# Attention values as the stationary operand, with the two terms moved through two column halves of the array

## What is computed

```python
scores = ttt_filter(q @ k.T / 8)                # [1024, 1024] per head
attn = softmax(scores)
attn = attn * (sin(C1*attn) * exp(-attn*attn/PHI) + cos(C2*attn))
ctx = attn @ v                                  # [1024, 64]
h = h + concat(ctx) @ Wo + bo
```

## Time and profile before

| | |
|---|---|
| runs shown, us | 6780.7, 6791.86, 6778.62 |
| time of the profiled execution, us | 6774.6 |
| its span, us | 6772.9 |
| mean granted TensorE clock | 0.892 of 2.4 GHz |
| TensorE matmul busy, us | 5442.1 (80%) |
| weight load busy, us | 3955.2 (58%) |
| VectorE busy, us | 5082.3 (75%) |
| ScalarE busy, us | 4262.2 (63%) |
| GpSimd busy, us | 2754.5 (41%) |
| of it GpSimd's sum L377, 1024 of 1272 ns, us | 1289.3 |
| values matmuls L635, 8192 records, busy us | 1162.6 |

### The profile page before, as it was taken

One profiled execution on the slowest core, in us unless ns is written; L12 is line 12 of the kernel. 1 busy time (PEld: TensorE's weight loads), 2 busy tenths in 40 slices (PEclk: granted clock), 3 DMA queues, 4 the chain that ended last, 5 costly groups with the idle time before them and its releaser, 6 DMA issues. The chain is left out here.

```text
span 6772.9 us, 115321 instructions
## 1 busy us (share of the span) xinstructions
PE 5442.1 (80%) x32426; PEld 3955.2 (58%) x32489; DVE 5082.3 (75%) x10177; ACT 4262.2 (63%) x7370; POOL 2754.5 (41%) x2639
## 2 busy tenths in 40 slices
PE   2788877787777877877888777778787799997999
PEld 1455555555555555555655555555555577775777
DVE  1888888888888888888888888888888555555443
ACT  1677777777777777777777777777777322222222
POOL 4445554444555544444555444445554200100111
PEclk9888898989889888888888889888988799898999
DMA  1000000000000000000000000000000000000000
GB/s 17 12 8 7 7 7 7 7 7 10 7 7 7 7 7 7 7 9 9 7 7 7 7 7 7 9 9 7 7 7 4 8 1 2 1 1 13 4 6 6
DMA packets 34500, 48.46 MB, mean 7 GB/s; under 512 B 24473, under 2 KB 24537, under 8 KB 34010
## 3 DMA queue, kind: packets, MB, share of 16 engines
q1 hardware_dynamic: 31962, 43.49, 2.5%
q0 software_dynamic: 2048, 0.14, 0.1%
HBM read 39.40 MB, written 4.19 MB: 6 GB/s over the span
## 5 line engine op out<-in xcount | busy, mean ns | idle before, releaser
L571 PE MATMUL banks<-ident,att 128*128 128x128 f32 x8192 | 1458.9, 311 | 873.6 <-DVE ag L508 496.8
L571 PEld LDWEIGHTS banks<-ident,att 128*128 128x128 f32 x8192 | 1024.2, 159 | 1568.6 <-DVE ag L508 1044.0
L377 POOL TENSOR_TENSOR sinb<-sinb,work 128x512 f32<-128x512 f32 x1024 | 1289.3, 1272 | 900.3 <-DVE sinb L482 898.3
L599 PE MATMUL banks<-kT,qT 128*128 128x512 f32 x2048 | 1262.5, 702 | 113.9 <-ACT att L423 104.0
L387 POOL TENSOR_SCALAR wgt<-wgt 128x512 f32<-128x512 f32 x1024 | 700.2, 684 | 1586.7 <-DVE wgt L502 1581.4
L635 PEld LDWEIGHTS outp<-vo,sinb 128*128 128x128 f32 x8192 | 1164.7, 216 | 214.9 <-issue 185.3
L635 PE MATMUL outp<-vo,sinb 128*128 128x64 f32 x8192 | 1162.6, 295 | 1.9 <-ACT att L423 1.9
L476 DVE TENSOR_TENSOR work<-banks,work 128x512 f32<-128x512 f32 x1024 | 699.8, 689 | 254.0 <-ACT work L435 183.6
L451 ACT ACTIVATE work<-banks 128x512 f32<-128x512 f32 x1024 | 609.9, 596 | 420.4 <-PE banks L571 411.6
L458 ACT ACTIVATE mag<-banks 128x512 f32<-128x512 f32 x1024 | 606.4, 594 | 356.2 <-PE banks L599 350.0
L435 ACT ACTIVATE work<-banks,halfpi 128x512 f32<-128x512 f32 x1024 | 695.4, 685 | 208.9 <-PE banks L571 139.6
(11 more groups left out here) (194 smaller groups left out, 6740.6 us busy)
## 6 DMA issues: line engine op xcount, KB each, us to landing
xq<-xT_dram SPq DMA_DIRECT2D x64, 256.0 KB
xv<-xT_dram SPq DMA_DIRECT2D x64, 256.0 KB, 3.7
xT_dram<-xT SPq DMA_DIRECT2D x8, 256.0 KB, 2.9
out<-hres SPq DMA_DIRECT2D x8, 256.0 KB, 2.6
base<-in_L_tok_turns,idx POOLq DMA_INDIRECT x64
wqk<-in_L_attn_Wq SPq DMA_DIRECT2D x64, 16.0 KB
wqk<-in_L_attn_Wk SPq DMA_DIRECT2D x64, 16.0 KB
wqk<-in_L_attn_bq SPq DMA_DIRECT2D x64, 0.2 KB
```

The costliest lines, as they stand in the source:

```text
L377: nc.gpsimd.tensor_tensor(sinb[:, k % RING], sinb[:, k % RING], work[:, k % RING], ALU.add).then_inc(summed, 1)
L571: mm = nc.tensor.matmul(bank[:, i * P:(i + 1) * P], att[:, p, 4 * half + i, kt * P:(kt + 1) * P], ident[:], is_transpose=True, start=(i == ...
L599: nc.tensor.matmul(score_bank(n), qT[:, p, (n // 2) * P:(n // 2 + 1) * P], kT[:, p, (n % 2) * 512:(n % 2 + 1) * 512], start=True, stop=Tru ...
```

## The change

- The values matmuls swap operands: `vo[:, kt]` (128x64) is stationary, and 512 columns are moved, once from `work` (cosine term) and once from `sinb` (sine term). The first writes partitions 0 to 63 of `outp`, the second 64 to 127: the built program gives them the tile 128x64 of the array at column 0 and at column 64. `outp` then holds output features by queries, for one half of the queries at a time.
- GpSimd's sum L377 is gone. ScalarE and VectorE wait for `av` where they waited for `summed`.
- The tiles go through the keys of the first query half, then of the second: `kt = k % TB`, `half = k // TB`. `AV` is one per step for the first eight (steps 34 to 41), every second step for the last eight (steps 0, 2, ... 14 of the next iteration).
- VectorE empties `outp` twice per head (steps 42 and 15): copied into `acc` for an even head, added to `acc` for an odd one. After the odd head TensorE folds `acc` back with eight 128x64 matmuls against `pair` (two stacked identities), and VectorE adds the result to `hres`. `PROJ` moves from step 18 to 19.
- `qT` and `kT` are no longer padded. Even heads lie on partitions 0 to 63, odd heads on 64 to 127, and the score matmul contracts 64 rows (tile 64x128 of the array, at row 0 or 64).

```diff
-        AV = [SINE + 6 + 8 * k // 5 for k in range(NTILE)]
-        OUT = AV[-1] + 1
+        AV = [SINE + 6 + k if k < TB else SINE + 16 + 2 * (k - TB) for k in range(NTILE)]
+        OUT = (AV[TB - 1] + 1, AV[-1] + 1)
+        FOLD, ADD = OUT[1] + 1, OUT[1] + 2
...
-                            wait(pool, tmul, NTILE * g + k + 1)
-                            nc.gpsimd.tensor_tensor(sinb[:, k % RING], sinb[:, k % RING], work[:, k % RING],
-                                                    ALU.add).then_inc(summed, 1)
...
-                        if a == OUT:
-                            wait(dve, av, NTILE * (g + 1))
+                        if a in OUT:
+                            half = OUT.index(a)
+                            wait(dve, av, NTILE * g + TB * (half + 1))
+                            if p == 0:
+                                nc.vector.tensor_copy(acc[:, half], outp[:]).then_inc(evac, 1)
+                            else:
+                                nc.vector.tensor_tensor(acc[:, half], outp[:], acc[:, half], ALU.add).then_inc(evac, 1)
+                        if a == ADD and p == 1:
+                            wait(dve, folded, folds(g, p) + 1)
...
-                            nc.tensor.matmul(score_bank(n), qT[:, p, (n // 2) * P:(n // 2 + 1) * P],
-                                             kT[:, p, (n % 2) * 512:(n % 2 + 1) * 512],
+                            rows = slice(p * D, (p + 1) * D)
+                            nc.tensor.matmul(score_bank(n), qT[rows, (n // 2) * P:(n // 2 + 1) * P],
+                                             kT[rows, (n % 2) * 512:(n % 2 + 1) * 512],
...
-                            wait(pe, summed, NTILE * g + k + 1)
+                            kt, half = k % TB, k // TB
+
+                            wait(pe, acd, NTILE * g + k + 1)
+                            wait(pe, tmul, NTILE * g + k + 1)
                             if k == 0:
                                 wait(pe, v_sb, g + 1)
-                            kt, half = k // 2, k % 2
-                            for i in range(4):
-                                o = (4 * half + i) * D
-                                mm = nc.tensor.matmul(outp[:, o:o + D], sinb[:, k % RING, i * P:(i + 1) * P],
-                                                      vo[:, kt, :], start=(k == 0 and i == 0),
-                                                      stop=(k >= NTILE - 2), skip_group_check=True)
+                            if k == TB:
+                                wait(pe, evac, 2 * g + 1)
+                            for term, rows in ((work, slice(0, D)), (sinb, slice(D, P))):
+                                mm = nc.tensor.matmul(outp[rows], vo[:, kt, :], term[:, k % RING],
+                                                      start=(kt == 0), stop=(kt == TB - 1), skip_group_check=True)
                             mm.then_inc(av, 1)
+                        if a == FOLD and p == 1:
+                            wait(pe, evac, 2 * g + 2)
+                            for j in range(TB):
+                                mm = nc.tensor.matmul(outp[:, j * D:(j + 1) * D],
+                                                      acc[:, j // 4, j % 4 * P:(j % 4 + 1) * P], pair[:],
+                                                      start=True, stop=True)
+                            mm.then_inc(folded, 1)
```

More of the change, by code:

```diff
@@ L277, in lattice @@
         names = ("consts loadq loadv projd qk_sb vald v_sb qk mags rounded kept factor filtered bias expd "
-                 "recip weights weights2 turned xpose squared gauss agd cosd acd nned sined tmul summed av outd").split()
+                 "recip weights weights2 turned xpose squared gauss agd cosd acd nned sined tmul av evac folded outd").split()
         (consts, loadq, loadv, projd, qk_sb, vald, v_sb, qk, mags, rounded, kept, factor, filtered, bias,
-         expd, recip, weights, weights2, turned, xpose, squared, gauss, agd, cosd, acd, nned, sined, tmul, summed,
-         av, outd) = (sem("l_" + n) for n in names)
+         expd, recip, weights, weights2, turned, xpose, squared, gauss, agd, cosd, acd, nned, sined, tmul,
+         av, evac, folded, outd) = (sem("l_" + n) for n in names)
         NTILE = 2 * TB
@@ L316, in stages, with folds @@
                     yield g, (par - stage) % 2, s + STEPS * stage
+        def folds(g, p):
+            if isinstance(g, int):
+                return g // 2
+            return (g - p) // 2
         def score_bank(n):
@@ L365, in _ @@
             pool.wait_ge(consts, 5)
-            nc.gpsimd.memset(qT[D:P], 0.0).then_inc(consts, 1)
-            pool.wait_ge(consts, 6)
-            nc.gpsimd.memset(kT[D:P], 0.0).then_inc(consts, 1)
+            nc.gpsimd.tensor_tensor(pair[:], ident[:, 0:D], ident[:, D:P], ALU.add).then_inc(consts, 1)
             def iteration(t, par):
@@ L401, in projections @@
                 cols = slice(c * 512, (c + 1) * 512)
-                nc.scalar.activation(qT[0:D, p, cols], outp[0:D], ACT.Copy, scale=QSCALE).then_inc(qk_sb, 1)
-                nc.scalar.activation(kT[0:D, p, cols], outp[D:P], ACT.Copy).then_inc(qk_sb, 1)
+                rows = slice(p * D, (p + 1) * D)
+                nc.scalar.activation(qT[rows, cols], outp[0:D], ACT.Copy, scale=QSCALE).then_inc(qk_sb, 1)
+                nc.scalar.activation(kT[rows, cols], outp[D:P], ACT.Copy).then_inc(qk_sb, 1)
             projections(0, 0, 0)
@@ L433, in iteration @@
                             else:
-                                wait(act, summed, NTILE * g + k - RING + 1)
+                                wait(act, av, NTILE * g + k - RING + 1)
                             nc.scalar.activation(work[:, k % RING], sine_bank(k), ACT.Sin,
@@ L447, in iteration @@
                             if d < RING:
-                                wait(act, summed, NTILE * g - RING + d + 1)
+                                wait(act, av, NTILE * g - RING + d + 1)
                             else:
@@ L549, in _, with project @@
         def _(pe):
-            pe.wait_ge(consts, 7)
-            def project(g, c):
+            pe.wait_ge(consts, 6)
+            def project(g, p, c):
                 wait(pe, loadq, 80 * (g + 1))
                 if c == 0:
-                    wait(pe, outd, g - 2)
+                    wait(pe, evac, 2 * (g - 2))
+                    wait(pe, outd, folds(g - 2, p))
                 else:
@@ L582, in iteration @@
                             wait(pe, acd, NTILE * g + k + 1)
[L583 to L584 removed]
+                            wait(pe, turned, TB * g + 4 * (k // TB) + 4)
+                            kt, half = k % TB, k // TB
                             for i in range(4):
@@ L643, in iteration @@
                             wait(pe, qk_sb, 4 * NHEADS if last else 4 * (g + 3))
-                            wait(pe, outd, g)
+                            wait(pe, evac, 2 * g)
+                            wait(pe, outd, folds(g, p))
                             for j in range(TB):
```

25 lines of the change are left out of this document (13 added, 12 removed).

## The result

The changed kernel takes 7798.2 us (median of 4 runs, 7772.48 to 7812.4), against 6779.66 us for the kernel before (4 runs): a ratio of 1.1495, 95% interval 1.1461 to 1.1528. It is 15% slower; the forecast was 3.5% slower, with 7290 us as the upper end of the range.

What follows compares the result with a forecast made beforehand. VectorE was taken to bound scores, gauss and the softmax's end, ScalarE the earlier softmax, no full engine the sine stretch. Terms summed to +3.7 us a head, 64 times +237 us on 6780.7, 7018 us; range 6770 to 7290 us.

Steps and rivals of the forecast that it cites:

- likeliest case: The forecast of 7018 us, with three slots a values tile: 6980 to 7080 us; chance 0.38.
- point 1: Sine stretch: eight steps with values matmuls take 2.01 us of TensorE instead of 1.56, +3.6 us a head.
- Point 7: Gauss stretch: 0.3 us drain per score matmul, mostly hidden in TensorE's idle time; +0.2 us a head.
- The end of the text: Signs to look for in the profile after; gauss stretch growing by several us would mean the forecast is wrong.
- Points 2 to 6: Sine steps losing values matmuls -0.3, emptying outp +0.4, step 0 +0.1, softmax values 0, residual add +0.3 us a head.
- point 8: After the softmax: without GpSimd's sums its scalings come earlier and VectorE's first rounding is quicker, -0.6 us a head.
- Point 5: Softmax and its end: seven tiles of values matmuls hidden while ScalarE, then VectorE, is the bound; cost 0.
- Point 9: Gauss stretch: new tile order lets first transposes go earlier, but VectorE is full, so it gives nothing by itself.
- serial: Rival for the values matmuls: the column halves run one after another, +7.3 us a head, 7248 us; chance 0.22.
- faster: Rival: halves overlap wholly, score drain hidden, GpSimd gives its full 1.0; -0.4 us a head, 6755 us; chance 0.10.

Runs made afterwards that it cites:

- padded kernel: Changed kernel with queries and keys padded with zero rows to 128 again, both query halves collected in one half of acc: 6935.77 us, ratio 1.0234.
- 64 and 65 rows: Kernel before with the score matmul reading only 64 rows of the padded queries and keys: 7885.86 us; the same edit with 65 rows: 7405.19 us.
- one-half experiment: Both terms written to partitions 0 to 63, against the changed kernel with 128-row scores and whole computation (7073.11 us): 7554.4 us, ratio 1.1123.
- one line of the table: Kernel before with values matmuls moved later, AV[k] = SINE + 9 + 7k // 5: 6742.72 us, ratio 0.994.
- the next step too far: Kernel before with values matmuls moved later still, AV[k] = SINE + 10 + 4k // 3: 6828.91 us, ratio 1.0075.

## Why the prediction was wrong

The direction held and the size did not: 15% instead of 3.5%. The padded kernel shows what the forecast was about: with the clock out of the way the change costs 2.3%, 6936 us, 44 us under the 6980 to 7080 us of the likeliest case. So the direction isn't luck, but the term that was to give nearly all of the loss, point 1, gives about 115 of the 1019 us (8 x 0.22 us in 64 heads), and one that was put at 0.2 us a head gives most of it. By its own points:

- **Point 7 failed, and it carries the miss.** I gave the 64-row scores 0.3 us of drain each, found 0.42 us of idle time to hide it, and took +0.2 us a head. I took the granted clock of the stretch (0.95 in the earlier trace rows) as given. With 64-row scores it stayed at 1.2 GHz for most of the stretch, which grew from 29.6 to 45.2 us; padding them again in the changed kernel gave back 862 us, which is 13.5 us a head. The end of the text named the sign of it (the gauss stretch growing by several us), but no rival priced it, so the range ended 500 us short. The zero rows that the change removed were not without use.
- **The drain itself** was sized right for 2.4 GHz. Where TensorE does not wait, a step from transpose to transpose takes 1.64 us in the changed kernel (2500.82 to 2502.46) and 1.36 us in the padded one (2509.12 to 2510.48): 0.28 us against the 0.3 of the prediction. And it is hidden there, as the step of 2.21 us shows. At 1.2 GHz TensorE is the bound, nothing hides it, and it is 0.49 us a step, the 481 us between 64 and 65 rows.
- **Point 1** had the sign and half of the size. I took three slots, 1.29 us a tile. Both terms run wholly beside each other, pass by pass, and the tile takes 1.01 us: 0.86 of passes and 0.15 more, with another 0.05 at the transposes ahead of it (0.53 us to the next start instead of 0.48). I had taken the 128x64 shape as free from the row of the transposes. Between tiles that follow each other with nothing else between, as in the softmax, the passes start 0.43 us apart (2488.47 to 2488.90), so the 0.20 us come only beside the 128x128 instructions. The step is 1.78 instead of 2.01 us, so the term is 8 x 0.22 = +1.8 us a head instead of +3.6. My argument that a second pass must hold up the other half was wrong: the trace has the passes interleaved. The Trainium skill, TensorEngine Tiling (Array Packing), Tiling Modes, states that different tiles run in parallel, which the 0.01 us between the two terms agree with, and that a change of mode drains the engine, which agrees with the 0.20 us here and the 0.28 us at the scores, but not with the 128x64 transposes of the earlier trace rows.
- **Points 2 to 6** were not measured one by one. The padded run is 160 us over before, 2.5 us a head; after the 1.8 us of point 1 they and point 8 leave 0.7, where the prediction had 0.4 + 0.1 + 0.3 - 0.3 - 0.6 = -0.1. Point 5 (values matmuls in the softmax are covered) rests on the clock too: in a softmax of the changed kernel at 0.54 TensorE has no time left to cover them, on its row by stretch:

```profile
2584.70:2600.70 16.00, 15.31 (x31) 3.62 (x32) 10.35 (x23) 12.69 (x21) 8.89 (x8) 0.54 0.00 1
```

- **Point 8 held** in its sign. Without the sums, VectorE's first rounding after the softmax takes 0.43 us in the padded kernel instead of 1.04, on its timeline below. From the kernel before to the padded one the mean over all 16 roundings of a head fell from 517 to 500 ns, and over the 8 roundings to whole turns from 858 to 822 ns, together 0.6 us a head of VectorE's busy time. What it gave in time no run shows.

```profile
2503.25 0.43 DVE L509 TENSOR_SCALAR wgt<-mag 128x512 f32<-128x512 f32 x1 [1.54 <-ACT mag L463]
```

- **Point 9 held**, by the two runs with the order of the tiles alone.

The rival "serial" is the one-half experiment, and the rival "faster" had the overlap right and the time wrong, as every rival had.

## What to carry to other kernels

A row of zeros that only fills a matmul up to 128 rows can be paying for itself through TensorE's clock: before taking it out, look up the granted clock of the stretch and redo the sum with TensorE at 1.2 GHz, where work that was hidden becomes the bound. Two fp32 products of 512 columns whose outputs go to different column halves took 1.01 us here where one alone takes 0.86 and both in one half 1.86, with the two standing next to each other in the order. That alone doesn't make the change pay: the padded kernel has it and is still 2.3% slower than the one before, whose values matmuls took 0.84 us a tile. And where an engine is the bound only in some stretches, moving its work by a few steps in the issue order can beat a rewrite: here one line of the table gave 0.6%, and the next step too far lost 0.75%.

## What the runs showed of the hardware

- TensorE was granted 1.2 GHz through 31.35 us in which it was busy all the time (the changed kernel's window from 2514.95 us), with 64-row scores. With 128-row scores, after the same 2.37 us wait, it was back at 2.4 GHz 9 us later. The Trainium skill, TensorE: Matmul & The Clock Gate, section on the clock gate (Part 1), ties the clock to how busy the engine has been. Here the busy share doesn't tell it: with 128, 96, 65 and 64 contracted rows in the scores the mean clock was 0.892, 0.841, 0.702 and 0.689, and the busy share of TensorE 80, 84, 89 and 90%. The rows that the three narrower forms leave out held only zeros. So it was the number of contracted rows that mattered, zeros included.
- The two passes of fp32 matmuls in different column halves interleave: first with first and second with second, 0.01 us apart.
- Between 128x128 instructions a pair in 128x64 tiles cost 0.15 us beyond its passes and 0.05 us at the transposes ahead, while 128x64 transposes had cost nothing visible. A 64x128 score matmul with the transposes around it cost 0.28 us more per step than a 128-row one at 2.4 GHz, and 0.49 us more than a 65-row one at 1.2 GHz.
